# Graph attention layer 1 with ten dense node tiles instead of thirteen, and fifteen summed edge by edge

## The reference, cut to what matters

```
def _gat(x, src, dst, W, a_src, a_dst, b, heads, ch, concat):
    h = (x @ W).reshape(n, heads, ch)
    es = (h * a_src).sum(-1)
    ed = (h * a_dst).sum(-1)
    e = leaky_relu(es[src] + ed[dst], 0.2)
    w = exp(e - segment_max(e, dst)[dst])
    alpha = w / segment_sum(w, dst)[dst]
    out = segment_sum(h[src] * alpha[:, :, None], dst)
    return out + b            # heads concatenated, or their mean
h = relu(layernorm(gat(x, ..., heads=4, ch=64)))      # layer 1
out = gat(h, ..., heads=1, ch=256)                    # layer 2
```

## Time and profile before

| | us |
|---|---|
| median of 3 runs (lowest, highest) | 1467.63 (1463.01, 1470.23) |
| the profiled execution, its own time | 1464.53 |
| its span, first to last instruction | 1462.6 |
| mean granted TensorE clock | 0.926 |
| busy over the span: PE, DVE, ACT, POOL | 1248.2 (85%), 866.2 (59%), 670.4 (46%), 775.4 (53%) |

### The profile page before, as it was taken

How to read it: one execution, slowest core, us unless ns; L and a number is a source line. 1 busy time by engine, 2 the same in 40 slices (tenths; PEclk the granted TensorE clock), 3 DMA queues, 4 the chain that set the end, 5 groups by cost and what they waited for, 6 DMA issues and landing times.

```text
span 1462.6 us, 21659 instructions
## 1 busy us (share of the span) xinstructions
PE 1248.2 (85%) x6282; PEld 957.9 (65%) x6283; DVE 866.2 (59%) x2590; ACT 670.4 (46%) x1758; POOL 775.4 (53%) x682
## 2 busy tenths in 40 slices
PE   2667799989999999767798897884599999999997
PEld 1446455545555655355686676773599999999996
DVE  7679798788799877634565774766722222222221
ACT  0348676656667777532243232331033334334432
POOL 4500578676767771056666665740444445444444
PEclk9779899999999999967899998986699999999999
DMA  7002743643553481233464554433033332323221
GB/s 239 5 18 87 198 118 100 177 119 101 163 140 105 139 231 31 102 117 97 149 192 129 180 170 123 139 100 107 8 86 89 99 95 43 91 39 92 38 36 26
DMA packets 138724, 157.86 MB, mean 108 GB/s; under 512 B 60020, under 2 KB 117729, under 8 KB 138649
## 3 DMA queue, kind: packets, MB, share of 16 engines
q0 software_dynamic: 35488, 75.68, 21.1%
q1 hardware_dynamic: 101056, 79.93, 17.7%
q10 hardware_dynamic: 2104, 1.38, 0.4%
HBM read 123.00 MB, written 34.70 MB: 108 GB/s over the span
## 4 chain that ended last, share of the span: by engine, by line
PE 59%; DVE 20%; issue 9%; DMA 4%; ACT 3%; another core or an unknown queue 3%; ACTq 1%; POOL 1%; DVEq 0%; POOLq 0%; SPq 0%
PE bank L1285 12%; PE bank L1403 11%; PE bank L1411 11%; PE bank L1236 9%; PE bank L1357 7%; DVE ring_a L1896 3%; DVE ohk L1618 2%; DMA out_x<-ring_a,si 2%; PE bank L1268 2%; DVE ohs L1614 1%; PE bank L1144 1%; PE bank L1169 1%; ACT ring_a L1017 1%; DVE st L1499 1%
## 5 line engine op out<-in xcount | busy, mean ns | idle before, releaser
L772 POOL DMA_INDIRECT arena<-rows,idx_e x385 | 430.0, 1117 | 254.6 <-issue 91.8
L1285 PE MATMUL bank<-ring_a,slots 128*65 128x384 f32 (+1 forms) x1000 | 333.2, 458 | 35.9 <-DVE ring_a L1896 31.0
L1017 ACT ACTIVATE ring_a<-vbb,slots 128x384 f32<-128x384 f32 (+1 forms) x500 | 243.8, 562 | 14.7 <-DMA vbb<-v_rows 10.9
L1285 PEld LDWEIGHTS bank<-ring_a,slots 128*65 128x65 f32 x1000 | 131.4, 143 | 154.5 <-issue 99.3
L1896 DVE SCALAR_TENSOR_TENSOR ring_a<-ring_a,arena 128x1536 f32<-128x1536 f32 (+1 forms) x125 | 192.1, 1538 | 20.0 <-ACT ring_a L1017 13.4
L1114 ACT ACTIVATE ring_a<-bank,cols 128x128 f32<-128x128 f32 x432 | 128.9, 371 | 160.5 <-PE bank L1403 160.2
L1357 PE MATMUL bank<-h2t,ring_a 128*128 128x257 f32 x650 | 179.3, 416 | 24.6 <-issue 14.1
L1236 PE MATMUL bank<-arena,ring_a 128*128 128x257 f32 (+1 forms) x770 | 193.6, 400 | 5.0 <-issue 3.8
L1236 PEld LDWEIGHTS bank<-arena,ring_a 128*128 128x128 f32 x770 | 154.3, 202 | 42.6 <-issue 12.3
L1357 PEld LDWEIGHTS bank<-h2t,ring_a 128*128 128x128 f32 x650 | 129.2, 208 | 49.1 <-issue 20.7
L823 POOL DMA_INDIRECT gs<-gates,gk x54 | 51.4, 953 | 149.1 <-DVE gk L2046 143.4
(11 more groups left out here) (297 smaller groups left out, 1678.6 us busy)
## 6 DMA issues: line engine op xcount, KB each, us to landing
counts_all<-arena SPq DMA_DIRECT2D x13, 800.0 KB
arena<-counts_all SPq DMA_DIRECT2D x13, 800.0 KB
arena<-in_L_ffn_W SPq DMA_DIRECT2D x8, 1024.0 KB, 7.5
vbb<-v_pairs SPq DMA_DIRECT2D x23, 320.0 KB
arena<-rows,idx_e POOLq DMA_INDIRECT x385
XB<-general_sums SPq DMA_DIRECT2D x38, 130.0 KB
vbb<-in_L_ffn_W SPq DMA_DIRECT2D x4, 1024.0 KB
spare<-in_L_ffn_W SPq DMA_DIRECT2D x4, 1024.0 KB
```

What stands on the lines that cost most here:

```text
L772: pool.indirect_dma_start(to[:, k, 0:width], None, table, bass.IndirectOffsetOnAxis(idx_e[:, m * PAIR + k:m * PAIR + k + 1], 0)).then_inc( ...
L1017: ins = act.activation(S1[q % SLOTS1][:, h * k * P:(h + 1) * k * P].rearrange("p (t n) -> p t n", n=P), vb1[:, 0:k, h, :], ACT.Copy, scale ...
L1285: pe.matmul(bank[h][0:CH + 1, 0:w_], slots[:, s, h * (CH + 1):(h + 1) * (CH + 1)], S1[q % SLOTS1][:, h * w_:(h + 1) * w_], start=(s == 0), ...
```

## The change

`NE` = 10 is the number of dense tiles of layer 1, `ND` = 13 stays that of layer 2. Layer 1 has four blocks, `Q1` = 100 steps, and `PAIRS` = 58 pairs (290 gathers), summed at steps 27 to 97 instead of 46 at steps 28 to 112. Layer 2 keeps its 13 dense tiles and 46 pairs (`PAIRS2`) at the same steps; it uses the index columns from pair 12 (`SKIP`) on. The counts of tiles 10 to 12 are still made during steps 75 to 98 (`CB` is the old list of blocks) and stored, but used in layer 2 alone. `load_counts(0)`, which stood at step 103 of 125, and `load_counts(1)` now both stand at step 102, two steps after the last summing step, behind a wait for all stores of counts. GpSimd waits for these stores too before layer 2. The plan's steps are now: tiles 22, 23 and 24 have their norm at 98 to 100 and their turns at 108, 110, 112; tiles 7, 8, 9 have spreads at 101, 103, 105, norms at 104, 106, 108, turns at 114, 116, 118; `END1` = 126. Before, only tiles 10, 11, 12 had their turn after the last summing step (spreads 126, 128, 130, turns 136, 138, 140). `orow` gets a sixth row so that the edge tiles' normalised rows rotate over three.

```diff
-ND = 13
-DW = ND * PER_TILE
-B1 = ((0, 1),) + tuple((t, min(3, ND - t)) for t in range(1, ND, 3))
+NE, ND = 10, 13
+EW, DW = NE * PER_TILE, ND * PER_TILE
+CB = ((0, 1),) + tuple((t, min(3, ND - t)) for t in range(1, ND, 3))
+B1 = CB[:1 + NE // 3]
...
-PAIRS = (NW - DW) // 2
+PAIRS, PAIRS2 = (NW - EW) // 2, (NW - DW) // 2
+SKIP = PAIRS - PAIRS2
...
-PAIR1 = [28 + p * 86 // PAIRS for p in range(PAIRS)]
-PAIR2 = [3 + p * 160 // PAIRS for p in range(PAIRS)]
+PAIR1 = [27 + p * 72 // PAIRS for p in range(PAIRS)]
+PAIR2 = [3 + p * 160 // PAIRS2 for p in range(PAIRS2)]
...
-    for t in range(ND, NT, 2):
+    for t in range(NE, NT, 2):
...
+def edge_row(t):
+    return 3 + (t - NE) % 3
...
-        orow = sb("orow", [P, 5, D])
+        orow = sb("orow", [P, 6, D])
...
-                if q % NT == 1 and 0 < q // NT < len(B1):
+                if q % NT == 1 and 0 < q // NT < len(CB):
                     store_counts(q // NT)
...
-                if q == (len(B1) - 1) * NT + 3:
+                if q == Q1 + 2:
                     for par in range(2):
-                        sp.wait_ge(s_cst[par], 16 * sum(B1[b][1] for b in range(par, len(B1), 2)))
-                    sp.wait_ge(s_a, (len(B1) - 1) * NT)
+                        sp.wait_ge(s_cst[par], 16 * sum(CB[b][1] for b in range(par, len(CB), 2)))
+                    sp.wait_ge(s_a, Q1)
                     load_counts(0)
-                if q == Q1:
-                    sp.wait_ge(s_a, Q1)
                     load_counts(1)
...
-                m = n % PAIRS
-                before = n - ROW_SLOTS[n // PAIRS] if m >= ROW_SLOTS[n // PAIRS] else -1
+                m = pair_of(n)
+                before = n - ROW_SLOTS[n >= PAIRS] if (n if n < PAIRS else n - PAIRS) >= ROW_SLOTS[n >= PAIRS] else -1
...
             pool.memset(ring_a[:, W2_AT:W2_AT + P // PW * W_PAIR], 0.0).then_inc(s_wz, 1)
+            for par in range(2):
+                pool.wait_ge(s_cst[par], 16 * sum(CB[b][1] for b in range(par, len(CB), 2)))
             pool.wait_ge(s_ht, 16 * NT)
...
             sums_out(len(B1) - 1)
             while q < END1:
+                for w, v, u in VISITS_AT.get(q - 2, ()):
+                    if v == VISITS - 1:
+                        window_out(w)
                 for p in PAIR1_AT.get(q - 2, ()):
                     pair_out(p)
...
-                        o, s_done = orow[:, 3 + i, :], s_oe
+                        o, s_done = orow[:, edge_row(t), :], s_oe
```

More of the change, by code:

```diff
@@ L82 @@
 assert max(GROUP_N) <= P and DW * VISITS <= 512 and PAIR * P <= (PAD_ROWS - ROWS) * P
-assert LOOP_ROWS <= ND and (NW - DW) % 2 == 0
+assert LOOP_ROWS <= NE and (NW - EW) % 2 == 0 and B1[-1][0] + B1[-1][1] == NE
 assert MAX_TILES + NT + 1 <= SLOT_TILES
@@ L100 @@
 _u = N_FIRST
-for _b in range(1, len(B1)):
+for _b in range(1, len(CB)):
     for _n, (_w, _v) in enumerate(visits_of(_b)):
@@ L166, in plan2 @@
     groups = [Group(range(t0, t0 + k), True, NT * (j + 1)) for j, (t0, k) in enumerate(B2)]
-    groups += [Group([t], False, PAIR2[last_pair(t)] + 2) for t in EDGE_TILES]
+    groups += [Group([t], False, PAIR2[last_pair2(t)] + 2) for t in EDGE_TILES]
     groups.sort(key=lambda g: g.end)
@@ L183 @@
 G1, G2 = plan1(), plan2()
+def edge_row(t):
+    return 3 + (t - NE) % 3
+for _t in range(NE, NT - 3):
+    _g, _h = (next(g for g in G1 if t in g.tiles) for t in (_t, _t + 3))
+    assert _g.turn[_g.tiles.index(_t)] - 1 < _h.norm[_h.tiles.index(_t + 3)]
+for _b in range(len(B1) - 1):
+    _g, _h = (next(g for g in G1 if B1[b][0] in g.tiles) for b in (_b, _b + 1))
+    assert max(_g.turn) - 1 < min(_h.norm)
 ORDER1 = [t for g in G1 for t in g.tiles]
@@ L587, in slot_of, with pair_of @@
             return GL2[k], s_g[k], 16 * PAIR * (before + (n - PAIRS) // ROW_SLOTS[1] + 1)
+        def pair_of(n):
+            return n if n < PAIRS else n - PAIRS + SKIP
         def block_of(t):
-            return next(b for b, (t0, k) in enumerate(B1) if t0 <= t < t0 + k)
+            return next(b for b, (t0, k) in enumerate(CB) if t0 <= t < t0 + k)
         def tiles1(b):
-            return range(B1[b][0], B1[b][0] + B1[b][1])
+            return range(CB[b][0], CB[b][0] + CB[b][1])
         def bank_of(use):
@@ L678, in _ @@
                     else:
-                        after(sp, s_oe, t - ND - 1)
+                        after(sp, s_oe, t - NE - 1)
                         sp.dma_start(XE[:, i, 1, :], gen[t * P:(t + 1) * P, :]).then_inc(s_ge1[i], 16)
@@ L703, in _ @@
                     rows = slice(0, P if t < NT - 1 else LAST)
-                    after(sp, s_on, ND + e - 1)
+                    after(sp, s_on, NE + e - 1)
                     sp.dma_start(XB[:, e % 2, 1, :], gen[t * P:(t + 1) * P, :]).then_inc(s_gl2[e % 2], 16)
@@ L795, in _ @@
             pool.wait_ge(s_gen, 2)
-            for n in range(PAIRS + ROW_SLOTS[1], 2 * PAIRS):
+            for n in range(PAIRS + ROW_SLOTS[1], PAIRS + PAIRS2):
                 gather_rows(n, rows2, T2W)
@@ L869, in window_out @@
                 act.wait_ge(s_vis, (w + 1) * VISITS)
-                if b >= 2 and w == B1[b][0] * PER_TILE:
+                if b >= 2 and w == CB[b][0] * PER_TILE:
                     act.wait_ge(s_a, (b - 1) * NT)
-                    act.wait_ge(s_cst[b % 2], 16 * sum(B1[a][1] for a in range(b % 2, b - 1, 2)))
-                i, wi = t - B1[b][0], w % PER_TILE
+                    act.wait_ge(s_cst[b % 2], 16 * sum(CB[a][1] for a in range(b % 2, b - 1, 2)))
+                i, wi = t - CB[b][0], w % PER_TILE
                 act.activation(C1[b][:, :, i * P + wi * WIN:i * P + (wi + 1) * WIN],
@@ L1050, in hooks2 @@
                     e = E2[t]
-                    after(act, s_on, ND + e - 1)
+                    after(act, s_on, NE + e - 1)
                     if g.dense:
@@ L1120, in _ @@
             pe.wait_ge(s_F, 1)
-            for g, (first, step) in enumerate(((0, 1), (DW, 2))):
+            for g, (first, step) in enumerate(((0, 1), (EW, 2))):
                 n = GROUP_N[g]
@@ L1792, in hits @@
             def hits(n, first):
-                p = n % PAIRS
+                p = pair_of(n)
                 after(v, s_pw, n)
@@ L1873, in hooks1 @@
                     after(v, s_T, NT + e - 3)
-                    o = orow[:, i, :] if g.dense else orow[:, 3 + i, :]
+                    o = orow[:, i, :] if g.dense else orow[:, edge_row(t), :]
                     v.tensor_scalar(xn[:, e % 4, :], o, mv[:, t, 0:1], rstd[:, t:t + 1], ALU.subtract, ALU.mult).then_inc(s_xn, 1)
```

32 lines of the change are left out of this document (17 added, 15 removed).

## The result

The changed kernel takes 1505.66 us (median of 4 runs, 1502.48 to 1507.48) beside 1467.91 us of the kernel before on the same chip (4 runs). The ratio is 1.0239, with a 95% interval of 1.0208 to 1.027: 37.8 us slower. The forecast was 1478, some 10 us slower, and its range, 1448 to 1506, holds the time just at its upper end. The profiled execution took 1505.95 us, its span is 1504.3 us, 41.7 us more than that of before.

What follows compares the result with a forecast made beforehand. TensorE set the pace before; after the change GpSimd's 290 gathers would bound layer 1. Its steps' end at +3.1 us and +7 behind them gave +10.1: 1474.6 profiled, 1477.7 for the median, said as 1478, range 1448 to 1506.

Steps and rivals of the forecast that it cites:

- The first gather: Start of GpSimd's gathers in layer 1, claimed unchanged at 151.7 us.
- The train: GpSimd's 290 gathers in layer 1 with their gaps and surplus, claimed to take 433.5 us, 1.495 us a gather.
- The hold: Layer 1 gathers wait for VectorE's long two-SBUF-input multiply: 0.82 us of GpSimd per instruction, 69 us in all.
- The buffer waits: GpSimd waiting for TensorE to free a row buffer in layer 1: 8 us, chosen between 0 and 42.
- From the last gather to the last matmul: Serial end of layer 1's steps: landing, weights, one-hots, a norm and a last TensorE step, 19.2 us.
- The tail: Behind layer 1's last step six tiles turn instead of three: +7 us, bounds 3 and 14.
- SyncE's 0: SyncE's stores of counts and loads before layer 2 fit: 0 us, up to 5 if tile 9's rows queue.
- Layer 2: Layer 2 keeps the same steps, so its time was claimed to change by 0 us.
- Rival B: Layer 1 gathers keep their old mean of 1.277 us, train ends at 617: +34 us, 1502; chance 22%.
- Rival A: Layer 1's gathers are not the bound, TensorE decides with 400 us for its work: -42 us, 1426; chance 8%.
- Rival C: VectorE's long instruction holds fewer layer 1 gathers, period 1.43 us: -9 us, 1459; chance 15%.
- the signs named ahead: Layer 1: buffer waits under 15 us, VectorE waiting tens of us, TensorE near 82% busy, last gather near 593.

Runs made afterwards that it cites:

- a_one: Changed kernel with the step's multiply by the counts replaced by an equally long VectorE instruction with one SBUF input (computation left out): 1403.75 us, ratio 0.9969 to the kernel before.
- fewer3: Changed kernel with only three of five gathers issued per pair from layer 1's fourth pair on (computation left out): 1388.08 us, ratio 0.9807 to the kernel before.
- a_slots: Changed kernel with four buffers of gathered rows in layer 1 instead of three: 1425.46 us, ratio 1.0093 to the kernel before.
- b_slots: Kernel before the change with four buffers of gathered rows in layer 1 instead of three: 1409.12 us, ratio 1.0005 to the kernel before.
- the control: Changed kernel run unaltered on the chips of the experiments: 1447.34 us, ratio 1.0265 to the kernel before.
- b_one: Kernel before with the multiply by the counts replaced by an equally long one-SBUF-input instruction (computation left out): 1400.90 us, ratio 0.9936 to the kernel before.
- n12_slots: Changed kernel with 12 dense tiles in layer 1 instead of 10, and four row buffers: 1393.63 us, ratio 0.9883 to the kernel before.

## Why the prediction was right in direction and short in size

**The first gather** comes 3 us earlier than said, 148.7 against 151.7. In the experiments too this mark moves by several us between kernels, with the first step.

**The train: a forecast of 433.5 us, 442.2 measured.** The gathers' own time came out at 355.2 instead of 277.5 + 69 = 346.5: the surplus over 0.957 us is 77.7 us, not 69. The hold is what the prediction said it was (the a_one pair: same instruction time, no hold), and it kept its price roughly: a gather that begins inside the instruction costs 68.1/66 = 1.03 us more, 68.3/73 = 0.94 before. The counts were a little off. 72 of L1922 stand in the train, not 76, and 87 in that of before, not 90; to them come 66 gathers that begin inside, 73 before. The rest of the surplus, 9.5 us instead of 5.2, is at other instructions. A term 9 us too small.

**The buffer waits: 8 us forecast, 28 measured. This is the step that failed.** The sentence was that "a bound engine doesn't wait", and the slack beside it was judged from TensorE's 5.4 us a pair against GpSimd's 7.5. TensorE's busy time alone is not what the other engines need. fewer3 shows that they need 427 us from step 25 on when gathers hardly matter, for 386 of which TensorE is busy; the train of gathers alone needs 450. So a bound engine does wait: two stages within some 5% of each other, coupled by three buffers, wait for each other in turn. With a fourth buffer the waits are 2 us and the kernel 22 us faster, as a_slots shows. That the unevenness comes from block changes, window ends and landings is argued, not tested. The size of the error is 20 of the 27 us by which the last gather came later (620.3 against 593.2).

**From the last gather to the last matmul: 19.2 us forecast, 21.5 measured.** Near enough.

**The tail: +7 forecast, +5.1 measured**, in the bounds of 3 to 14. From the last matmul to layer 2's first step before took 30.0 us and after takes 35.1 (641.8 to 676.9). The chain splits it against that of before, of which two rows:

```profile
612.40 4.36 DMA XB<-general_sums
...
623.29 1.74 PE bank L1268 x4
```

The first to the last turn takes 14.5 us instead of 7.4, +7.1, near the 8.5 that three more turns could cost. **SyncE's 0 was a little wrong:** the load of the general sums starts 4.6 us after the last matmul instead of 3.1, for the issue of the last block's counts (L677) and a store of rows (L717) stand ahead of it in the chain, 3.7 us from the one to the load, which makes +1.5 us against before. The landing and the norm before the first turn were shorter by 0.8 and 2.4 us, which the prediction didn't see. The counts themselves arrive in time.

**Layer 2: 0 forecast, +3.7 measured** (365.8 to 369.5 us from its first step to its last matmul), and +3.2 on the other chips between b_slots and the control. No run was made for its cause; it stays open.

**Rival B gave 1502 and came closer to the time than the forecast, but its mechanism is not what happened.** It wanted a mean of 1.277; the mean is 1.225 and the missing time is in the waits. That the range holds the time is luck, for its upper end was set by rival B; the forecast's own range ended at 1489. A reader who took the number as proof would have gone after the hold alone, and missed the 22 us of the fourth buffer. **Rival A**, the gathers not the bound, falls with fewer3. Its price of 400 us for the other engines was 27 us too low; of the 427, TensorE stands still for 41, where rival A had carried over 21 from before. The Trainium skill (Perfetto Trace Analysis, Identifying the Most-Contended Engine) has the engine with the highest occupancy improved first, but says of TensorE that its matmul busy share is no good measure of how near it is to its limit. The prediction left that exception out. Read by busy share alone, taking work off TensorE with its 94% should have gained; the kernel lost 38 us. b_one and b_slots show that layer 1's steps gain nothing in that kernel from faster gathers or one more buffer either. Both engines stand near the bound, and shifting work helps only as far as n12_slots goes. **Rival C**, fewer holds, falls with the mean.

Of the signs named ahead: VectorE's waits for gathers in tens of us came (80.6), TensorE's share of 82% came (83%), GpSimd's waits under 15 us did not (28), nor the last gather near 593 (620).

## What to carry to other kernels

When work moves from the bound engine to another, price the second engine's stretch by its start and end with all gaps, and measure how long the rest needs without it (leave part of the suspected work out): busy shares of 94% and 72% were, once the work had moved, two stages only some 5% apart. Two stages so close can wait for each other through their buffers, so it pays to try a move that makes them equal with one more buffer, and in several sizes; here one tile moved together with a fourth buffer gained 1.2%, three tiles with three buffers lost 2.4%.

## What the runs showed of the hardware that I had not expected

- A gather that begins inside the two-input VectorE instruction ends 0.83 us past that instruction's end (median of 66). Splitting it in four back to back takes only a quarter of what one input instead of two takes (means 1.213 to 1.156, against 0.994), while the four keep VectorE busy 12% longer than the one.
- Two sets of chips run the same kernel at 1468 and 1409 us, and most of it is in layer 2 (395.8 us between two marks on the first, 347.3 on the others in b_slots, the kernel before with one more row buffer in layer 1), while ratios agree (1.0239 and 1.0265). Why was not tested.
- The first step of layer 1 comes between 89.5 and 103.8 us in kernels whose work before it is the same, so a difference of some us in the total says little without the marks.
